# Correlation attention: bias added row by row, fewer steps behind the means, circulants loaded from two queues before the barrier, mirrored values made earlier

## The reference

```
q = (layernorm(x) @ Wq + bq)   # heads split; k, v from ctx_1024
k = (keys @ Wk + bk);  v = (values @ Wv + bv)
corr = jnp.fft.irfft(q_fft * jnp.conj(k_fft), n=Lq, axis=-1)
mean_value = corr.mean(axis=(1, 2))                       # (16, 128): one value per shift
_, index = jax.lax.top_k(mean_value.mean(axis=0), TOP_K)
weights = mean_value[:, index]
tmp_corr = jax.nn.softmax(weights, axis=-1)
idx = (jnp.arange(Lq)[None, :] + index[:, None]) % Lq
gathered = v[..., idx]
agg = jnp.einsum('bhekl,bk->bhel', gathered, tmp_corr)
out = agg.transpose(0, 3, 1, 2).reshape(Bq, Lq, Dq)
return out @ Wo + bo        # then x = x + tanh(g_xattn[3]) * this
```

## Time and profile before

| | |
|---|---|
| median of 3 runs | 956.03 us (952.27 to 965.45) |
| profiled execution | 957.7 us, its span 955.9 us |
| span before the correlation block | 745.8 us |
| walk of the correlation block | 745.8 to 778.7 us |
| chain behind the means | 778.7 to 786.8 us |
| bias on POOL, barrier | 786.8 to 791.7 us |
| wait for the circulants | 791.7 to 794.9 us |
| rows of the roll block until POOL's first send | 794.9 to 804.4 us |
| sends | 804.4 to 849.4 us |
| expert layer and output | 849.4 to 955.9 us |

### The profile page before, as it was taken

How to read it: one execution, slowest core, us unless ns; L and a number is a source line. 1 busy time by engine, 2 the same in 40 slices (tenths; PEclk the granted TensorE clock), 3 DMA queues, 4 the chain that set the end, 5 groups by cost and what they waited for, 6 DMA issues and landing times. The chain is left out here.

```text
span 955.9 us, 21238 instructions
## 1 busy us (share of the span) xinstructions
PE 804.1 (84%) x6318; PEld 607.5 (64%) x6318; DVE 603.4 (63%) x1841; ACT 510.3 (53%) x1423; POOL 415.1 (43%) x705
## 2 busy tenths in 40 slices
PE   4999996997579999999978974999988856869992
PEld 1466664796457777777755762666658634639992
DVE  5799985343456777777655435899957745743333
ACT  1466664674046656656643651677764422316663
POOL 2356655001524456655333006566517414743442
PEclk9999998899599999999998985799998977569996
DMA  8999910342000000000002441000000222122214
GB/s 277 377 409 405 314 52 30 84 95 55 17 6 13 10 16 25 18 19 18 13 15 67 111 109 29 18 19 19 13 1 2 62 73 81 46 61 55 69 55 148
DMA packets 69278, 78.96 MB, mean 83 GB/s; under 512 B 12848, under 2 KB 58560, under 8 KB 68912
## 3 DMA queue, kind: packets, MB, share of 16 engines
q1 hardware_dynamic: 60256, 62.74, 20.7%
q0 software_dynamic: 6368, 13.38, 4.8%
q10 hardware_dynamic: 2544, 1.48, 0.6%
HBM read 31.61 MB, written 45.96 MB: 81 GB/s over the span
## 5 line engine op out<-in xcount | busy, mean ns | idle before, releaser
L324 POOL DMA_INDIRECT routed_region<-routed_lines,line_slots x96 | 96.6, 1006 | 27.8 <-issue 22.4
L356 POOL DMA_INDIRECT late_results<-routed_region,line_slots x64 | 63.5, 992 | 80.4 <-DVE work L639 64.2
L1340 PE MATMUL banks<-exps,work 128*128 128x128 f32 x624 | 85.6, 281 | 5.3 <-ACT exps L1414 5.1
L891 PE MATMUL banks<-work,weights_a 128*128 128x128 f32 x512 | 77.4, 296 | 14.0 <-ACT work L1121 8.2
L259 POOL TENSOR_TENSOR small<-small,half_and_eps 128x1 f32<-128x1 f32 x144 | 83.8, 582 | 11.3
L773 ACT ACTIVATE probs_keymajor<-banks 128x512 f32<-128x512 f32 x128 | 69.9, 595 | 34.0 <-PE banks L569 34.0
L1340 PEld LDWEIGHTS banks<-exps,work 128*128 128x128 f32 x624 | 77.9, 196 | 7.6 <-ACT exps L1414 7.3
L644 DVE TENSOR_REDUCE small<-banks 128x8 f32<-128x1024 f32 x64 | 77.6, 1212 | 7.9 <-PE banks L543 7.7
L543 PE MATMUL banks<-work 32*128 32x512 f32 x256 | 81.7, 718 | 0.0
L653 DVE TENSOR_TENSOR exps<-banks,small 128x1024 f32<-128x1024 f32 x64 | 77.7, 1214 | 3.8 <-PE banks L569 3.4
L891 PEld LDWEIGHTS banks<-work,weights_a 128*128 128x128 f32 x512 | 65.2, 199 | 23.1 <-ACT work L1121 10.2
(11 more groups left out here) (283 smaller groups left out, 1932.8 us busy)
## 6 DMA issues: line engine op xcount, KB each, us to landing
routed_region<-mid SPq DMA_DIRECT2D x52, 528.0 KB, 5.4
exps<-routed_region SPq DMA_DIRECT2D x125, 66.0 KB, 2.0
routed_region<-work SPq DMA_DIRECT2D x86, 64.0 KB, 1.8
weights_f<-in_weights_f SPq DMA_DIRECT2D x1, 4096.0 KB, 17.4
weights_f<-in_weights_f SPq DMA_DIRECT2D x3, 1024.0 KB, 11.1
shifted_rows<-work SPq DMA_DIRECT2D x16, 128.0 KB, 1.7
work<-expert_results SPq DMA_DIRECT2D x8, 256.0 KB, 4.5
routed_region<-routed_lines,line_slots POOLq DMA_INDIRECT x96, 2.4
```

Source lines behind the costliest of these rows:

```text
L324: nc.gpsimd.indirect_dma_start(k.regions[layer % 2], bass.IndirectOffsetOnAxis(k.slots[:, b, j:j + 1], 0), k.line[:, b % LINES, j, :], Non ...
L356: nc.gpsimd.indirect_dma_start(k.late[:, b % 2, j, :], None, k.regions[layer], bass.IndirectOffsetOnAxis(k.slots[:, b, j:j + 1], 0)).then_ ...
L891: last = nc.tensor.matmul(bank[:, MA, p * T:(p + 1) * T], k.w[weight][:, p * 128:(p + 1) * 128], kvT[:, sl, part * T:(part + 1) * T], star ...
L1340: last = nc.tensor.matmul(bank[:, 2 + m % 4, i * T:(i + 1) * T], tile.weights[:, m % COPIES, i * 128:(i + 1) * 128], tile.gotT[:, m % 2, : ...
```

## The change

- POOL adds the bias to row b (128 by 128) in the walk, as a stage `bias` with lag 2 behind `dev_in`, once row b is normalised. The one large addition goes.
- Behind the means, the average stays in its bank and is read from there by three operations. The tie's count is folded into a per-row scalar, the selection and the penalty into two `scalar_tensor_tensor` operations, and the sign is turned so that ACT's exponential subtracts the extreme value through its bias and scale. The division moves to the last operation, which writes `cr2`.
- The four circulant loads are issued in `correlation_block`, parts 0 and 2 by SP and parts 1 and 3 by ACT, behind the arrival of `circulant_rows` and ahead of the barrier. Their semaphores become lasting ones (`ld.circ`).
- The 16 products with the mirror leave the roll block's walk. They stand in `correlation_block` in four groups of four: two between the last means, one behind the tie's ranks, one at the end. ACT copies each group with one instruction of 128 by 512 into the second half of `exps`.

The core of the diff:

```
+            def mirror(q):
+                for b in range(4 * q, 4 * q + 4):
+                    last = nc.tensor.matmul(bank[:, q, (b % 4) * T:(b % 4 + 1) * T], c["mirror"], at(vtok, b),
+                                            start=True, stop=True)
+                last.then_inc(s.vm, 1)
+            def mirrors(b, sl):
+                if b == B - 2:
+                    pe.wait_ge(s.qk_out, B)
+                    pe.wait_ge(s.v, B)
+                if b >= B - 2:
+                    mirror(b - (B - 2))
-            walk(pe, [(products, 3), (in_T, 0), (project, 1), (means, 10)])
+            walk(pe, [(products, 3), (in_T, 0), (project, 1), (means, 10), (mirrors, 6)])
...
-            act.wait_ge(s.pen, 2)
-            nc.scalar.activation(ex, tmp, ACT.Exp, accum_out=rs[:, 0:1]).then_inc(s.ex, 1)
+            def mirrored_out(q):
+                act.wait_ge(s.vm, q + 1)
+                nc.scalar.activation(mirrored[:, 512 * q:512 * q + 512], bank[:, q, :], ACT.Copy).then_inc(s.vs, 1)
+            mirrored_out(0)
+            mirrored_out(1)
+            act.wait_ge(s.pen, 1)
+            nc.scalar.activation(ex, tmp, ACT.Exp, bias=least[:, 0:1], scale=-1.0, accum_out=rs[:, 0:1]).then_inc(s.ex, 1)
+            mirrored_out(2)
+            mirrored_out(3)
+            act.wait_ge(s.sent_c, 16)
+            load_circulants(act, (1, 3))
...
-            walk(pool, [(dev_in, 0)])
-            pool.wait_ge(s.xh, B)
-            pool.wait_ge(s.cr2, 1)
-            nc.gpsimd.tensor_tensor(k.x[:, :, :], k.x[:, :, :], over(k.tgb[:, 2, :], B, 1), ALU.add).then_inc(s.biased, 1)
+            def bias(b, sl):
+                wait(pool, s.xh, b + 1)
+                nc.gpsimd.tensor_tensor(at(k.x, b), at(k.x, b), k.tgb[:, 2, :], ALU.add).then_inc(s.biased, 1)
+            walk(pool, [(dev_in, 0), (bias, 2)])
...
             sp.wait_ge(s.sent_c, 16)
+            load_circulants(sp, (0, 2))
...
-            step(v.tensor_copy(gm, bank[0:B, 7, 0:T]))
+            gm = bank[0:B, 7, 0:T]
             step(v.max(top8, gm))
...
+            step(v.tensor_scalar(ties[:, 0:1], ngt[:, 0:1], -1.0, float(TOP_SHIFTS), ALU.mult, ALU.add))
+            step(v.tensor_scalar(below, gt, MASKED, -MASKED, ALU.mult, ALU.add))
             dve.wait_ge(s.rank, 1)
-            step(v.tensor_scalar(sel, bank[0:B, 7, 256:256 + T], ngt[:, 0:1], float(TOP_SHIFTS), ALU.add, ALU.is_lt))
-            step(v.tensor_tensor(sel, sel, eq, ALU.mult))
-            step(v.tensor_tensor(sel, sel, gt, ALU.add))
-            step(v.tensor_scalar(pen, sel, -MASKED, MASKED, ALU.mult, ALU.add))
+            dve.wait_ge(s.eq, 1)
+            step(v.scalar_tensor_tensor(sel, bank[0:B, 5, 256:256 + T], ties[:, 0:1], eq, ALU.is_lt, ALU.mult))
+            step(v.scalar_tensor_tensor(pen, sel, MASKED, below, ALU.mult, ALU.add))
             dve.wait_ge(s.m, 1)
-            step(v.tensor_tensor(tmp, m, pen, ALU.add))
-            v.tensor_reduce(mxv[:, 0:1], tmp, AX.X, ALU.max).then_inc(s.pen, 1)
-            dve.wait_ge(s.pen, 1)
-            v.tensor_scalar(tmp, tmp, mxv[:, 0:1], None, ALU.subtract).then_inc(s.pen, 1)
+            step(v.tensor_tensor(tmp, pen, m, ALU.subtract))
+            v.tensor_reduce(least[:, 0:1], tmp, AX.X, ALU.min).then_inc(s.pen, 1)
             dve.wait_ge(s.ex, 1)
             step(v.reciprocal(ri[:, 0:1], rs[:, 0:1]))
-            v.tensor_scalar(cw, ex, ri[:, 0:1], None, ALU.mult).then_inc(s.cw, 1)
...
-            v.tensor_copy(cr2, over(bank[0:B, 6, 256:256 + T], 2, 1)).then_inc(s.cr2, 1)
+            v.tensor_scalar(cr2, over(bank[0:B, 6, 256:256 + T], 2, 1), ri[:, 0:1], None, ALU.mult).then_inc(s.cr2, 1)
...
-            walk(pe, [(ranks, 6), (aggregate, 1), (logits, 5), (mirror, 0), (out, 1), (next_T, 4)])
+            walk(pe, [(ranks, 6), (aggregate, 1), (logits, 5), (out, 1), (next_T, 4)])
```

More of the change, by code:

```diff
@@ L1739, in correlation_block, with load_circulants @@
     r = w[0:B, 4096:8192]
-    m, gm, gt, eq, sel, pen, ex, cw, tmp = (r[:, 128 * n:128 * (n + 1)] for n in range(9))
+    m, gt, eq, sel, pen, ex, tmp, below = (r[:, 128 * n:128 * (n + 1)] for n in range(8))
     cr2 = split(r[:, 1280:1536], T)
-    top8, ngt, mxv, rs, ri = (r[:, 1536 + 8 * n:1544 + 8 * n] for n in range(5))
-    eqT, cwT = w[:, 6144:6144 + B], w[:, 6160:6160 + B]
+    top8, ngt, least, rs, ri, ties = (r[:, 1536 + 8 * n:1544 + 8 * n] for n in range(6))
+    eqT, exT = w[:, 6144:6144 + B], w[:, 6160:6160 + B]
+    circ = k.pT[:, :].rearrange("p (b t) -> p b t", b=B)
+    mirrored = k.e[:, 1, :]
+    def load_circulants(queue, parts):
+        for part in parts:
+            from_, to = PARTS[part:part + 2]
+            queue.dma_start(circ[:, from_:to, :], bass.AP(scratch_c.tensor, from_ * 2 * T,
+                                                          [[1, T], [2 * T, to - from_], [1, T]])).then_inc(ld.circ[part], 16)
     sn = norm_names(sems, "c3_in")
@@ L1776, in _ @@
             pe.wait_ge(s.eq, 1)
-            nc.tensor.transpose(bank[:, 7, 128:128 + B], eq, c["ident"][0:B, 0:B]).then_inc(s.eqT, 1)
+            nc.tensor.transpose(bank[:, 5, 128:128 + B], eq, c["ident"][0:B, 0:B]).then_inc(s.eqT, 1)
             pe.wait_ge(s.eqT_out, 1)
[L1779 to L1783, removed]
+            nc.tensor.matmul(bank[0:B, 5, 256:256 + T], eqT, c["earlier"], start=True, stop=True).then_inc(s.rank, 1)
+            mirror(2)
+            pe.wait_ge(s.ex, 1)
+            nc.tensor.transpose(bank[:, 6, 128:128 + B], ex, c["ident"][0:B, 0:B]).then_inc(s.exT, 1)
+            pe.wait_ge(s.exT_out, 1)
+            nc.tensor.matmul(bank[0:B, 6, 256:256 + T], exT, c["mirror"], start=True, stop=True).then_inc(s.cr, 1)
+            mirror(3)
         @block.scalar
@@ L1905, in roll_block @@
     circ = k.pT[:, :].rearrange("p (b t) -> p b t", b=B)
[L1906 removed]
+    agg, xs2 = (split(w[:, 256 * n:256 * (n + 1)], 128) for n in (1, 3))
     so = norm_names(sems, "r3_out")
@@ L1917, in _ @@
         def _(sp):
-            for part in range(4):
-                from_, to = PARTS[part:part + 2]
-                sp.dma_start(circ[:, from_:to, :], bass.AP(scratch_c.tensor, from_ * 2 * T,
-                                                           [[1, T], [2 * T, to - from_], [1, T]])).then_inc(s.circ[part], 16)
             sems.clear_last(sp)
@@ L1979, in _ @@
         def _(act):
-            def mirrored(b, sl):
-                wait(act, s.vm, b + 1)
-                wait(act, s.agg, b - 1)
-                nc.scalar.activation(vs[:, sl, :], bank[:, 7, 0:D], ACT.Copy).then_inc(s.vs, 1)
             def aggregated(b, sl):
```

43 lines of the change are left out of this document (19 added, 24 removed).

## The result

Twenty runs of each kernel on the chip gave 955.42 us as the median of the changed kernel and 960.89 us of the kernel before. The ratio is 0.9941, with a 95% interval of 0.9916 to 0.9967, so the change took 3.2 to 8.1 us off, less than two per cent. One of the changed kernel's twenty runs took 1301.23 us at a mean clock of 0.558 (the others have 0.89 to 0.91) and is left out of the ratio. The forecast was 951.4 us against a median before of 956.03, a difference of 4.6 us, in a range of 946 to 957. The median of twenty runs of the kernel before lies 4.9 us above the three that the forecast started from, and this is why 955.42 lies 4.0 us above the forecast although the difference came out larger than forecast. The profiled execution's span is 953.8 us, 2.1 us under the 955.9 of before.

A forecast was written before the change was run, and what follows sets the result against it. It took the chain of waiting small steps, then POOL's addition holding the barrier, as the bound. The terms 1.4 + 3.5 - 0.2 - 0.4 + 0.3 + 0.2 - 0.2 = 4.6 us off 956.03 gave 951.4 us, range 946 to 957.

The forecast's parts named there:

- The shift arrives as summed: Whole kernel: the first send's shift reaches the end, 4.6 us saved, own range 948 to 954.5 us; chance 0.62.
- Chain: Small steps behind the means: fewer steps and bank reads, and division moved off the path, save 1.4 us.
- Gap: From `cr2` to the first `aggregate`: 4.68 us instead of 8.16, 3.5 us saved if the barrier comes before part 0's landing.
- Part 0 may share engines with part 1: Circulant loads in the gap: two queues at once may delay part 0, 0 to 0.6 us, taken as 0.2.
- Bias in the walk: Correlation block's walk: POOL's 16 row additions slow DVE's normalisation beside them, 0 to 1.1 us, taken as 0.4.
- Or the walk longer than 33 us: Correlation block's walk: a sign listed for the prediction being wrong, beside L263 rows well over 0.35 us.
- Blocked DVE: Walk: each addition blocks DVE's normalisation for its full 0.40 us, walk grows 6.4 us, total 957.4 us; chance 0.08.
- Clock in the chain: Last mean and averaging: mirror products fill PE's wait and keep its clock high, 0 to 0.6 us saved, taken as 0.3.
- Roll block: Roll block's start: 0.2 us saved where row 0's ranks wait behind a mirror, 0.2 lost to a later clock rise.
- a clock of 0.50 through the roll block's first rows with the time to the first send over 10 us: Roll block's start: a sign listed for the prediction being wrong.
- Barrier or queue: Gap: a barrier or queue wait replaces the addition, saving 2.3 us instead of 3.5, total 952.6 us; chance 0.12.
- Quicker rows: Roll block: without mirrors the first rows go 0.43 us quicker each, 1.7 us more saved, total 949.7; chance 0.08.

The follow-up runs named there:

- e4: Changed kernel with the mirror products and copies back in the roll block's walk: chain 6.76 us, gap 5.31, roll start 9.47.
- e5: Changed kernel with all four circulant loads issued by SP in the order of the parts, none by ACT: gap 4.64 us.
- e1: Kernel before with only the bias added row by row by POOL in the walk: gap 5.11 us.
- e12: Changed kernel with the circulant loads put back behind the block's barrier, all from SP's queue: gap 5.55 us.
- e3: Kernel before with only the shorter chain of steps behind the means: chain 6.54 us.
- e7: Changed kernel with seven unread mirror products added, three behind `mirror(3)` and four ahead of the first `aggregate`: roll start 8.64 us.
- e11: Changed kernel measured again, same code, on the third chip: 966.19 us, ratio to before 0.9973.
- e2: Kernel before with only the four circulant loads moved ahead of the barrier, all from SP, large addition kept: gap 6.14 us.
- e9: Changed kernel with ten unread products added ahead of the walk's first row: walk 33.33 us.
- e10: Changed kernel with one load queue, a one-row first part, six fills around the roll block's start and six ahead of the walk: 965.51 us, ratio to before 0.9951.
- e8: Changed kernel with a second, unread addition per row on POOL: walk 36.18 us.
- e6: Changed kernel with all circulant loads from SP's queue and the first part cut from two rows to one: gap 4.49 us.

## Why the prediction was right, and where its steps were off

**The difference.** It said 4.6 us; the medians differ by 5.5, and the part of the profile that the change reaches shows 3.4. Both ratios measured, 0.9941 and 0.9973, have the predicted 0.9952 in their interval, but they would have 3.4 us in it as well. So the mechanism held and the sum was 1.2 us too large: the roll block fell short by 0.6, chain with clock by 0.2, gap by 0.2, bias by 0.1. That the medians nevertheless differ by more than 4.6 has no reason in the traces: on that side the forecast was lucky. "The shift arrives as summed" was the case that came by its stages; the 955.42 us lie above its own range (948 to 954.5), because the kernel before was measured slower too. The sends kept their length (44.04 and 44.09), as said: the shift passed on to the last send.

**Chain: 1.4 us, measured 1.26 for the steps.** Up to the exponential they save 1.00 us (5.47 to 4.47 from the copy of the means to its start, before and e4) where 0.17 + 0.87 was forecast. Behind it they save 0.26 and not 0.48: the exponential itself takes 0.40 us for 0.31, and `cr2` 0.47 and not 0.41. `mirror(2)`, "0 to 0.5, I take 0.1", cost nothing, as the transposition's start shows. The whole chain came to 1.47 us less, with 0.21 from the clock, below.

**Gap: 3.5 - 0.2 us, measured 3.07.** Right in kind, with one term too small. "Part 0 may share engines with part 1", 0.2 us, is 0.45 us (e5). But the sum reads as if the loads ahead were needed for it. The bias by row alone gives 3.05, because the barrier by itself is nearly free once POOL is out of it (0.4 us in e1, from the landing of `circulant_rows` to the first load). The loads ahead earn 0.91 us only because `mirror(3)` would hold the barrier (e12).

**Bias in the walk: 0.4 us, in a walk that grew by 0.53.** The price fits but is not shown, and the proof foreseen for it was no proof. The closest pair, e1 and e3, on one chip and with the same mean clock of 0.95 in the walk, differs by 0.44 us. But the walk of the changed kernel alone took 33.22 to 34.56 us in the traces that leave it as it is (e5 to e7, e11, e12, after), and without the bias it took 32.61 to 33.69 (before, e2, e3). "Or the walk longer than 33 us" came true with 33.39, but 0.37 of it is the clock at the start, which e2 has without any bias. From first to last scores the two best comparisons are 21.68 and 21.81 us without the bias (before, e3), and 21.82 to 22.27 with it (after, e1, e5 to e7, e9, e10, e11): 0 to 0.6 us. e2 without it has 22.37 and e4 and e12 with it 22.50 and 22.67, so the size isn't known better. Blocked DVE is out: the most that any L264 lost beside an addition of 0.45 us was 0.07. The Trainium skill's rule in "SBUF — State Buffer" (Who interferes with whom), that of two engines on the shared ports the second waits for the whole instruction of the first, did not show here; whether L264 runs in the two-port mode that the rule asks for, no run tells.

**Clock in the chain: 0.3 us, measured 0.21 in one trace and 0.42 in another of the same code.** With the new steps the chain takes 6.76 us where both the average and the ranks ran at the low level (e4), 6.54 or 6.55 where the average ran at the high one (after, e3, e8, e9, e10), and 6.32 or 6.33 where the ranks did so too (e5, e6, e7, e11, e12). The ranks in the changed kernel and in e11:

```profile
784.25 0.61 PE L1802 MATMUL banks<-consts,work 128*16 128x128 f32 x2 [0.49 <-DVE work L1910]
```

```profile
783.51 0.39 PE L1802 MATMUL banks<-consts,work 128*16 128x128 f32 x2 [0.55 <-DVE work L1910]
```

The forecast's reason, eight products in PE's wait ahead of the last means, fits: in all nine traces with them the average took 0.39 us, in the five without them 0.39 twice (e1, e3), 0.44 once (e2) and 0.60 twice (before, e4); the ranks took 0.39 in five of the nine and never without them. So the mirrors raise the odds and don't decide it; this is a count of single traces and no proof.

**Roll block: 0.2 - 0.2 = 0, measured 0.60 us longer.** This step failed most. It named the mechanism ("PE is less busy at the start, and its clock may rise later") and priced it for two to three products, 0.15 us. Before, with PE busy without a gap from the first `aggregate` on, the clock rose about 5 us behind it; busy times of the kernel before:

```profile
794.89:800.00 5.11, 5.11 (x20) 4.41 (x20) 1.96 (x8) 1.67 (x6) 0.29 (x1) 0.50 0.76 225
800.00:804.37 4.37, 3.72 (x27) 2.80 (x26) 3.89 (x19) 2.23 (x11) 1.11 (x3) 0.96 0.02 7
```

After, PE is busy 8.24 of 10.08 us, and the clock stays at 0.50 through this stretch and through the 44 us of the sends. The products on the way to the first send are more than three: each row is 1.6 us at the low level and 1.1 to 1.2 at the high one, and e7 bought 1.44 us with seven spare products. The sign foreseen for it, "a clock of 0.50 through the roll block's first rows with the time to the first send over 10 us", is what came: by the prediction's own list it stood under "wrong", and it cost 0.6 of the 4.6 us.

**Barrier or queue** did not come in the changed kernel, whose gap hangs on a transfer. It came in e10, by another way than forecast, through four issues on SP's own queue. **Quicker rows** did not come either: the rows became slower.

## What to carry to other kernels

Before several edits on one wait are summed, ask what the wait costs with each alone: two that remove the same stall don't add, and a third (here the mirrors moved in front of a barrier) can give the weaker one its worth. Products that fill a wait of TensorE are not free to move: here the clock went with them, and the rows that they left ran slower (e4, e7); price that over every product up to the next bound, not over a few. A first load that something waits for should go out ahead of its siblings from one queue (0.45 us here); making it smaller gained 0.15. And when a chain of small steps is timed, look at the duration of each product in it before the gain is put down to the steps: 0.21 us of 1.47 were the clock at one product.

## What the runs showed that I had not expected

- The landing of the first circulant load hardly depends on its size: from one queue 128 KB took 3.1 to 3.2 us, 64 KB 2.9 to 3.0.
- With one queue four issues took 1.93 us on SP (e10), 2.75 in e1; in e10 SP was late at its barrier by them.
- The walk's first 5 us had a mean clock of 0.81 in one trace and 0.56 in another, with the same code ahead of them and PE idle for 2.88 us ahead of its first product in both. What decides between the two was not settled.
- The sends took 44.0 to 44.1 us in six traces (before, after, e5, e6, e7, e9) and 46.7 to 48.4 in the eight on the two chips where the kernel before took 969 to 971 us; e11 and the changed kernel are the same code. In e11 POOL's own time per send is the same, but DVE's L289 releases it late:

```profile
L325 POOL DMA_INDIRECT routed_region<-routed_lines,line_slots x32 | 31.5, 986 | 13.4 <-issue 7.7 <-DVE line_slots L289 5.8
```

The cause stays open. These 2.6 to 4.4 us are part of the higher times on those chips.
